# A channel-mixing block in float32 on one core: units of two images' parts become units of one image's halves, with one joined GroupNorm chain per image and new step orders

## What is computed

```python
x = x + hadamard(gn(x))            # GroupNorm: 32 groups of 6 channels, per image, over all tokens
x = x + mlp(gn(x))
def mlp(h):                        # per token
    h = gelu(layernorm(h @ W1.T + b1, g1, beta1))
    h = gelu(layernorm(h @ W2.T + b2, g2, beta2))
    return h @ W3.T + b3
```

## Time and profile before

| | |
|---|---|
| time, median of 3 runs | 929.75 us (927.37 to 929.77) |
| span of the profiled execution, first to last instruction | 927.5 us |
| outside the span, against the median | 2.2 us |
| PE, ACT, DVE, POOL busy in the span | 831.8, 814.3, 799.5, 551.2 us |
| start of step 0, of step 7, of step 44, of `drain` (step 48) | 75.17, 210.70, 829.04, 889.66 us |
| six steps in the middle | 101.0 us |

### The profile page before, as it was taken

The page is one execution under the profiler, slowest core; times in us unless marked ns, Lnnn a source line. Parts: engine busy times, 40 slices in busy tenths (PEclk is TensorE's granted clock), DMA queues, the critical chain, the costliest instruction groups (busy, mean ns, idle before and its releaser), DMA issues.

```text
span 927.5 us, 22221 instructions
## 1 busy us (share of the span) xinstructions
PE 831.8 (90%) x8353; PEld 552.3 (60%) x8353; DVE 799.5 (86%) x1416; ACT 814.3 (88%) x2400; POOL 551.2 (59%) x414
## 2 busy tenths in 40 slices
...
GB/s 265 234 69 145 1 70 69 74 69 104 107 69 108 103 105 98 81 103 108 70 110 101 94 117 70 98 113 84 59 40 55 50 36 104 40 69 35 70 36 102
DMA packets 52090, 81.99 MB, mean 88 GB/s; under 512 B 14608, under 2 KB 14736, under 8 KB 51856
## 3 DMA queue, kind: packets, MB, share of 16 engines
...
...
## 4 chain that ended last, share of the span: by engine, by line
PE 48%; DVE 31%; ACT 10%; POOL 7%; issue 2%; SPq 1%; DMA 1%; ACTq 0%; DVEq 0%; POOLq 0%
PE tm L578 11%; DVE z L1248 6%; PE tm L573 5%; PE tp L590 5%; DVE X L1089 5%; DVE xs_lo L1080 4%; POOL ge_lo L943 4%; PE hl L487 4%; DVE bn L1106 3%; DVE x_lo L1230 3%; PE hl L418 3%; ACT z L729 3%; PE tm L567 3%; PE hl L516 2%; PE hl L492 2%; PE hl L511 2%
## 5 line engine op out<-in xcount | busy, mean ns | idle before, releaser
L943 POOL TENSOR_TENSOR ge_lo<-ge,ge_hi 128x512 f16<-128x512 f32 (+1 forms) x190 | 314.1, 1664 | 189.7 <-ACT ge_hi L759 189.7
L729 ACT ACTIVATE z<-tm 128x194 f32<-128x194 f32 x784 | 250.8, 346 | 41.9 <-PE tm L578 38.6
L935 POOL TENSOR_TENSOR rs<-ssq,neg_half 128x4 f32<-128x4 f32 x196 | 204.9, 1046 | 124.1 <-ACT z L729 123.2
L1248 DVE TENSOR_TENSOR z<-tm,rs 128x768 f32<-128x768 f32 x196 | 186.0, 949 | 62.1 <-POOL rs L935 61.3
L729 ACT ACTIVATION_READ_ACCUMULATOR z<-tm 128x1 f32 x784 | 175.1, 223 | 0.0
L741 ACT ACTIVATE ge<-tp,par 128x512 f32<-128x512 f32 x196 | 155.2, 792 | 21.1 <-PE tp L590 20.5
L759 ACT ACTIVATE ge_hi<-ge 128x512 f16<-128x512 f32 (+1 forms) x190 | 161.8, 855 | 2.9
L1089 DVE SCALAR_TENSOR_TENSOR X<-hl,h_bias,X 128x512 f32<-128x512 f32 x138 | 102.0, 741 | 30.6 <-PE hl L423 30.1
L590 PE MATMUL tp<-cst,z 128*128 128x128 f32 x784 | 121.8, 278 | 4.9 <-DVE z L1248 2.8
L1230 DVE SCALAR_TENSOR_TENSOR x_lo<-X,gscale,x_hi 128x512 f16<-128x512 f32 x144 | 102.8, 743 | 1.1 <-ACT x_hi L706 1.1
L590 PEld LDWEIGHTS tp<-cst,z 128*128 128x128 f32 x784 | 85.7, 142 | 28.4 <-issue 21.7
(11 more groups left out here) (192 smaller groups left out, 1888.2 us busy)
## 6 DMA issues: line engine op xcount, KB each, us to landing
...
out<-X SPq DMA_DIRECT2D x8, 64.0 KB, 3.0
```

Source lines behind the costliest of these rows:

```text
L729: last = nc.scalar.activation(z[n][:, 2 * h + k, i * TW:(i + 1) * TW], tm[h][:, i, k * TW:(k + 1) * TW], ACT.Square, scale=float(C) ** -0. ...
L935: nc.gpsimd.tensor_tensor(rs[n][:, 2 * h:2 * h + 2, :], ssq[n][:, 2 * h:2 * h + 2, :], neg_half[0:TT, 0:4].rearrange("p (i k) -> p i k", i=2),
L943: nc.gpsimd.tensor_tensor(ge_lo[n][:, g % 2, PART[h], :], ge[n][:, PART[h], :], ge_hi[n][:, g % 2, PART[h], :], ALU.subtract).then_inc(s_g ...
L1248: nc.vector.tensor_tensor(z[n][:, 2 * h:2 * h + 2, 0:2 * C].rearrange("p k (i o) -> p i k o", i=2), tm[h][:, :, 0:2 * TW].rearrange("p i ( ...
```

## The change

A unit is now the two *halves* of one image: 512 tokens from each half of 1536. So U = 3 units per image, N = 48 as before, and two of its three blocks belong to the same image and the same channels: they have the same scale, shift and bias, and ACT's and DVE's operations on them become one of 128 x 1024. `X` is a ring of RX = 14 units, refilled one unit at a time. The leftovers (64 tokens of each image) have tiles of their own, `XL`, `xsl_*`, `left*`; they stay in SBUF and are no longer stored and loaded back. There is one chain per image, which does the first norm of image q+2 and the second norm of image q together (19 chains with those of the start-up); its small operations are cut into stages that stand between other work. H_AHEAD is 4. The Hadamard stage of only four units stands ahead of step 0.

```diff
-U = 6
-N = U * PAIRS
+U = 3
+N = U * B
-H_AHEAD = U + 1
-FIRST_H = {1: (6, -1), 2: (7, 8), 3: (9, -1), 4: (10, 11)}
-FIRST_STATS = (7, 4, 3, 4, 0, 1, 4, 5, 5, 3)
-PERIOD_STATS = (4, 4, 3, 3, 2, 2)
-DPOS = 44
+H_AHEAD = 4
+AHEAD_STATS = 24
+FIRST_STATS = (5, 7, 0)
+PERIOD_STATS = (5, 4, 0)
+DPOS = N - 2
+LEFT_AT = {3 * q + 1: (q,) for q in range(B - 1)}
+def chain_images(j):     # (image of norm 1, image of norm 2)
+    if j < 4:
+        return ((0, None), (1, None), (None, 0), (2, None))[j]
+    q = j - 3
+    return (q + 2 if q + 2 < B else None), q
+def chain_at(g):
+    if g == 0:
+        return 3
+    q, r = divmod(g + 1, U)
+    return 3 + q if r == 0 and 1 <= q < B else None
...
             def residual(a, b):
+                if b == 0:
+                    dve.wait_ge(s_h, 2 * a + 1)
+                    nc.vector.scalar_tensor_tensor(out=X[:, a % RX, 0:2, :], in0=hl[:, :, 0:UT], scalar=bias[:, 0:1],
+                                                   in1=X[:, a % RX, 0:2, :], op0=ALU.add, op1=ALU.add).then_inc(s_res, 1)
...
             def h_left(a):
+                for k, terms in enumerate(((AA, CA_), (AC_, CCD))):
+                    for b, m in enumerate(terms):
+                        for r, part in enumerate(parts):
+                            last = nc.tensor.matmul(hl[:, 0, k * REM:(k + 1) * REM], h16[:, m, :], part[:, b, :], ...
...
+def run(first, steps, last, drain):
+    for g in range(NL + 2):
+        (drain if g >= NL - 1 else last if g >= N - H_AHEAD else steps[g % U] if g else first)(g)
```

The three kinds of step are `step` (g divisible by 3), `step_left` (`split_left`, `residual_left`, and the chain's aggregates at its end) and `step_norm` (the chain). DVE's part of the last is new:

```diff
+            def step_norm(g):
+                gn_stats(chain_at(g), 1)
+                residual(h_unit(g), 0)
+                stats_part(g, 0)
+                gn_stats(chain_at(g), 2)
+                stats_x1(h_unit(g), 0)
...
+                gn_var(chain_at(g), 2)
+                scaled_lo(h_unit(g + 1), 0)
+                gn2_shift(chain_at(g))
+                gn1_shift(chain_at(g), 0)
...
+                gn_h_bias(chain_at(g))
+                normalise(g - 1, 1, 1)
+                final_c(g - 2)
+                stats_x1(h_unit(g), 1)
+                stats_x1(h_unit(g), 2)
```

More of the change, by code:

```diff
@@ L22 @@
 GROUP = C // 32
[L23 to L25 removed]
+RX = 14
+RL = 4
 W_SCALE = 64.0
```

1317 lines of the change are left out of this document (716 added, 601 removed).

## The result

| | median us | range (runs) |
|---|---|---|
| kernel before | 928.7 | 927.4 to 929.8 (4) |
| changed kernel | 997.4 | 986.2 to 998.3 (4) |

The ratio is 1.071, 95% interval 1.065 to 1.076. The forecast was 911 us (897 to 927). The profiled execution has a span of 995.6 us.

A forecast was written before the change was run, and what follows sets the result against it. PE was taken to set the pace in the middle, with DVE half a step behind. Terms: 65.5 + 32.5 + 14 images x 50.7 + 62.7 + 37.8 = 908.3 us of span, a median of 911 us (897 to 927).

The forecast's parts named there:

- Term 1: Start-up, with DVE as its thread: falls from 75.2 to 65.5 us, bounds 61 to 71.
- Term 2: Steps 0 and 1, which lack part of the pipeline: 32.5 us together; seven steps come to 117 against 135.5.
- Term 3: Middle, steps 2 to 43: 50.5 to 50.7 us per image, bounds 50.0 and 52.2.
- Term 4: The end: last four steps 62.7 us, drain unchanged at 37.8, with 3 us either way.
- rule on DRAIN: Trainium skill: a semaphore costs DVE nothing extra; the forecast instead took 0.20 us for linked small operations, 0.08 for unlinked.
- Rival B: Norm step goes serial on one PSUM bank: 941 us if each of 15 loses 2.0 us more; chance 0.08.
- A: Staging saves nothing and DVE leads: 52.2 us per image, 921 to 932 us; chance 0.12 of 918 to 927, 0.03 same.
- C: PE runs through without idle: 50.0 us per image and a shorter drain, 899 us; chance 0.14.
- D: No start-up gain, as ACT holds the first group to 75: 920 us; chance 0.04.

The follow-up runs named there:

- e13: Changed kernel with GpSimd's gelu_lo subtracting only 2 columns of each block of 256 from group 2 on: 927.8 us, ratio 0.998.
- e3: Changed kernel with 7 dummy matmuls on TensorE ahead of its wait for gn_means in the norm steps: 976.6 us, ratio 1.051.
- e6: Changed kernel with the norm step reordered on VectorE, GpSimd and TensorE, gelu_lo waiting for the chain's shifts: 989.0 us, ratio 1.063.
- e11: Changed kernel with a second norm-step order, split_left_lo after residual_left, gelu_lo waiting for x1_split_lo, and the bias-row cast after two bn_stats: 947.4 us, ratio 1.020.
- e15: Kernel of e11 with gelu_lo shortened in the same way as in e13: 930.8 us, ratio 1.002.

## Why the prediction was wrong, step by step

- **Term 1, start-up 65.5 (61 to 71):** 69.04, inside its bounds; 66.1 to 69.6 in the variants. The first Hadamard matmul starts at 24.68, as forecast (24.8); the 3.5 us are missed behind it, where three small VectorE operations stand beside GpSimd's long splits (2.26, 1.74 and 1.67 us, at 32.0, 44.7 and 46.4).
- **Term 2, steps 0 and 1, 32.5:** 33.53. Step 7 starts at 197.99, not near 182: 4.5 us from these two terms, the other 11 from the norm steps 2 and 5 (22.07, 23.53) and the left step 4. The 12.7 us gained on the kernel before up to there (210.70) are real.
- **Term 3, 50.7 us per image: the step that failed.** It took 56.6 (792.94 / 14), with VectorE busy 92% of these steps, not over 98%. Plain 15.9 was right; left 16.5 and norm 18.3 were not. The sums of work were nearly right: with `gelu_lo` short the same instructions take 52.0 per image (727.71 / 14), plain 16.2 to 16.4, left 16.5 to 17.1, norm 18.8, inside the bounds of 50.0 to 52.2. The sentence that failed is "One that is waited for costs 0.20": in this order the chain's square takes 1.94 to 2.07 us in all 13 steady norm steps. I priced operations by rows in which no `gelu_lo` happened to stand ahead of one that it can hold, and never laid the new order of GpSimd beside that of VectorE. That GpSimd (POOL) "has a third of its time free" was the wrong question; what counts is when it is busy.
- **The sum again:** +3.5 start-up, +1.0 steps 0 and 1, +83.1 middle, -0.4 at the end, which is the 87.3 us. Of the 83.1, 65.2 go with GpSimd's long operations, and 17.9 are left without them (e13). Of these, 3.3 us are step 2, where e13's `gelu_lo` are still long (22.06 against 18.8 us); and in the norm steps the chain's root takes 1.97 us instead of the 1.01 of the earlier trace rows. How much of that lies on the path wasn't measured. e3 gives about 21 us to TensorE's lower clock, which fell behind the idle time in the norm step and stands within the 65.2. At the full clock the norm step 26 took 20.6 us, 1.8 more than with `gelu_lo` short. Per step the 65 are 3.6 us in a norm step (22.4 against 18.8) and 1.3 in a left step (18.1 against 16.8).
- **Term 4, 62.7 + 37.8:** 61.77 + 38.32. Right.
- **The rule on DRAIN:** the links stayed at 0.18 to 0.20 us wherever no `gelu_lo` ran (279.57 to 279.75), so row and forecast were right against that rule; it wasn't what decided.
- **Rival B** named the right step and sign, with the wrong mechanism and too small a price (2.0 per norm step; it was 4.1). The idle time it asked for before L348 or L361 isn't there; it stands before L335, ahead of `gn_means`. It did appear, 2.87 us at L348, when e6 moved `w1_shift` behind `l3_ab`. **A** (VectorE leads, 52.2) is about what e13 takes per image (52.0), though TensorE was the busier there (709.7 against 682.8 us). **C** and **D** didn't come about.

No version tried beats the kernel before. The best, e11, starts step 7 at 188.8 instead of 210.70, 22 us earlier, and gives back more in the middle: six steps take 105.96 us instead of 101.00. What of this another order could still avoid stays open. e15 bounds it for this order: GpSimd's long operations cost 16.6 us, none of it in the norm step, and that order's norm step (19.6) is 0.8 us longer than the changed kernel's with `gelu_lo` short (18.8).
